# Expert transposes issued two experts ahead, a 320-column first gate product, and the order around them

## What is computed

```python
scores = jax.nn.sigmoid(tokens @ router_w)          # 64 experts, 8 chosen per token
dispatch = dispatch.at[flat_e, pos_c].add(tokens[tidx] * valid[:, None])   # 256 slots per expert
g = jnp.einsum('ech,ehi->eci', dispatch, gate_w)    # 512 -> 256
u = jnp.einsum('ech,ehi->eci', dispatch, up_w)
expert_out = jnp.einsum('eci,eih->ech', jax.nn.silu(g) * u, down_w)
contrib = gathered * (topk_w.reshape(-1) * valid)[:, None]
output = jnp.zeros((t, h), tokens.dtype).at[tidx].add(contrib)
```

## Time and profile before

| | |
|---|---|
| median of 3 runs | 1308.94 us (1308.88 to 1310.11) |
| the profiled execution, its own time | 1307.97 us |
| its span | 1306.2 us, mean granted TensorE clock 0.996 |
| busy, whole span | PE 98%, DVE 70%, ACT 50%, POOL 33% |
| chain that ended last | PE 96% |

### The profile page before, as it was taken

How to read it: one execution, slowest core, us unless ns; L and a number is a source line. 1 busy time by engine, 2 the same in 40 slices (tenths; PEclk the granted TensorE clock), 3 DMA queues, 4 the chain that set the end, 5 groups by cost and what they waited for, 6 DMA issues and landing times.

```text
span 1306.2 us, 22561 instructions
## 1 busy us (share of the span) xinstructions
PE 1280.0 (98%) x7565; PEld 1123.8 (86%) x7565; DVE 916.0 (70%) x1787; ACT 647.3 (50%) x1053; POOL 433.9 (33%) x344
## 2 busy tenths in 40 slices
PE   6999999999999999999999999999999999999995
PEld 5888888888888888888889999999999999999994
DVE  7878877777777777785656667667766766676662
ACT  4421232212322123221256777777877777777772
POOL 1000000000000000000014666777666667676653
PEclk9999999999999999999999999999999999999998
DMA  7336554664546645445447999999999999999995
GB/s 269 121 107 163 130 121 127 157 166 98 130 119 153 167 104 131 114 118 134 134 133 214 286 278 286 287 290 292 290 291 285 298 291 287 282 295 285 298 277 65
DMA packets 203800, 263.65 MB, mean 202 GB/s; under 512 B 49268, under 2 KB 138744, under 8 KB 203768
## 3 DMA queue, kind: packets, MB, share of 16 engines
q1 hardware_dynamic: 175096, 191.93, 50.9%
q0 software_dynamic: 28672, 71.32, 23.7%
HBM read 178.18 MB, written 71.39 MB: 191 GB/s over the span
## 4 chain that ended last, share of the span: by engine, by line
PE 96%; DVE 2%; DMA 1%; ACT 0%; issue 0%; POOL 0%; SPq 0%; ACTq 0%
PE pmm L1255 18%; PE pmm L1257 18%; PE pmm L1256 18%; PE pout L1255 11%; PE pout L1257 11%; PE pout L1256 11%; PE ptr L1488 4%; PE plog L1316 2%; PE plog L1325 1%; PE ptr L1267 0%; DMA out_dram<-outs,slot_cols 0%; DVE stats L829 0%; DMA xbuf<-_L_attn_proj_matrix_dram 0%; DVE xt_lo L795 0%; PE plog L1345 0%
## 5 line engine op out<-in xcount | busy, mean ns | idle before, releaser
L1614 POOL DMA_INDIRECT out_dram<-outs,slot_cols x128 | 228.7, 1787 | 165.6 <-DMA out_dram<-outs,slot_cols 136.2
L1255 PE MATMUL pmm<-xt_hi,proj_hi 128*128 128x256 f32 (+1 forms) x784 | 253.0, 323 | 2.2 <-DVE xt_lo L795 1.4
L1257 PE MATMUL pmm<-xt_hi,proj_lo 128*128 128x256 f32 (+1 forms) x784 | 249.6, 318 | 0.0
L1256 PE MATMUL pmm<-xt_lo,proj_hi 128*128 128x256 f32 (+1 forms) x784 | 249.6, 318 | 0.0
L1255 PE MATMUL pmm<-xt_hi,sgu_hi 128*128 128x256 f32 (+1 forms) x768 | 246.1, 320 | 0.2 <-issue 0.2
L1256 PE MATMUL pmm<-xt_lo,sgu_hi 128*128 128x256 f32 (+1 forms) x768 | 243.4, 317 | 0.0
L1257 PE MATMUL pmm<-xt_hi,sgu_lo 128*128 128x256 f32 (+1 forms) x768 | 243.4, 317 | 0.0
L1598 POOL TENSOR_TENSOR earlier<-earlier,chosen 128x64 bf16<-128x64 bf16 x64 | 23.9, 373 | 617.8 <-DVE chosen L916 614.0
L1604 POOL DMA_INDIRECT xbuf<-rows,slot_cols x128 | 175.3, 1369 | 80.8 <-issue 38.6
L552 ACT ACTIVATE feat<-pmm,ab 128x512 f32<-128x512 f32 x68 | 46.7, 687 | 292.4 <-PE pmm L1257 286.4
L1255 PEld LDWEIGHTS pmm<-xt_hi,proj_hi 128*128 128x128 f32 x784 | 147.3, 188 | 13.6 <-ACT feat L552 1.6
(11 more groups left out here) (185 smaller groups left out, 2543.7 us busy)
## 6 DMA issues: line engine op xcount, KB each, us to landing
raw<-in_L_ffn_gate_w_dram SPq DMA_DIRECT2D x64, 512.0 KB
raw<-in_L_ffn_up_w_dram SPq DMA_DIRECT2D x64, 512.0 KB
raw<-in_L_ffn_down_w_dram SPq DMA_DIRECT2D x64, 512.0 KB
outs<-in_L_attn_x_dram SPq DMA_DIRECT2D x32, 512.0 KB, 3.9
out_dram<-outs SPq DMA_DIRECT2D x32, 512.0 KB, 3.0
xbuf<-in_L_attn_x_dram SPq DMA_DIRECT2D x52, 256.0 KB, 7.6
raw<-xn SPq DMA_DIRECT2D x52, 256.0 KB, 6.2
rows<-raw SPq DMA_DIRECT2D x39, 256.0 KB, 4.2
```

Of the source, the lines that this page charges most:

```text
L1255: pe.matmul(psum, lh, rh, start=first and n == 0, stop=False)
L1256: pe.matmul(psum, lh, rl, start=False, stop=False)
L1257: ins = pe.matmul(psum, ll, rh, start=False, stop=final and n == len(pairs) - 1)
L1614: pool.indirect_dma_start(out=out, out_offset=bass.IndirectOffsetOnAxis(ap=slot_cols[:, at:at + 1], axis=0), in_=outs[e.b][:, c, :], in_of ...
```

## The change

On TensorE the transposes of an expert are issued two experts ahead and stand between gate-and-up products and the down products; ScalarE and VectorE handle the transposed rows at the matching place. The first gate product of every expert covers 320 columns in place of 256 (the 64 further columns are written into PSUM that the next block of products overwrites). VectorE takes `down_lo` ahead of `e_hidden` and `slot_tokens` at the front of a stage; GpSimd issues each gather one addition sooner (`add_rows(n - 5)` follows `gather(n)`).

```diff
 # ScalarE, stage
-                if next_rows:
-                    e_turned_hi(e.next())
                 if next_weights:
                     gate_up_hi(e.next())
                 e_silu(e)
                 down_hi(e)
+                if next_rows:
+                    e_turned_hi(e.next().next())
                 e_hidden_hi(e)
 # ScalarE and VectorE, start: one more e_turned_hi/lo(turn(1)) ahead of stage(turn(0))
 # VectorE, stage
-                if next_rows:
-                    e_turned_lo(e.next())
+                if tokens is not None:
+                    slot_tokens(tokens)
                 if next_weights:
                     gate_up_lo(e.next())
+                down_lo(e)
                 e_hidden(e)
-                down_lo(e)
+                if next_rows:
+                    e_turned_lo(e.next().next())
                 e_hidden_lo(e)
-                if look is not None:
-                    look[0](look[1])
+                if blocks is not None:
+                    pass_blocks(blocks)
 # TensorE, products and e_gate_up
                 for n, (lh, ll, rh, rl) in enumerate(pairs):
-                    pe.matmul(psum, lh, rh, start=first and n == 0, stop=False)
+                    if n > 0 or not lead:
+                        pe.matmul(psum, lh, rh, start=first and n == 0, stop=False)
...
+                        lead = m == 0 and i == 0
+                        if lead:
+                            pe.matmul(pmm[m][:, 0:CAP + E_LEAD], egu_hi[e.b][:, at[0]],
+                                      xt_hi[e.b][:, 0, E_COLS.start:E_COLS.stop + E_LEAD], start=True, stop=False)
 # TensorE, the loop over experts
                     e = four(2 * m + 1, k)
-                    e_turn(e.next())
                     e_gate_up(e)
                     if k == 1:
                         look_up(m + 2)
+                    e_turn(e.next().next())
                     e_down(e.prev())
 # GpSimd
-                if n >= 4:
-                    add_rows(turn(n - 4))
+                if n >= 5:
+                    add_rows(turn(n - 5))
```

More of the change, by code:

```diff
@@ L58 @@
 E_COLS = slice(48, 48 + CAP)
+E_LEAD = 64
 class Turn:
@@ L753, in _ @@
             e_turned_hi(turn(0))
+            e_turned_hi(turn(1))
             stage(turn(0), next_weights=False, out_prev=False)
@@ L761, in _ @@
             for n in range(E - 6, E - 1):
-                stage(turn(n))
+                stage(turn(n), next_rows=n < E - 2)
             stage(turn(E - 1), next_rows=False, next_weights=False)
@@ L1224, in e_hidden_lo, with stage @@
                                   ALU.subtract).then_inc(e_hid_lo_made, 1)
-            def stage(e, next_rows=True, next_weights=True, look=None):
-                if next_rows:
-                    e_turned_lo(e.next())
+            def stage(e, next_rows=True, next_weights=True, tokens=None, blocks=None):
+                if tokens is not None:
+                    slot_tokens(tokens)
                 if next_weights:
                     gate_up_lo(e.next())
+                down_lo(e)
                 e_hidden(e)
-                down_lo(e)
+                if next_rows:
+                    e_turned_lo(e.next().next())
                 e_hidden_lo(e)
-                if look is not None:
-                    look[0](look[1])
+                if blocks is not None:
+                    pass_blocks(blocks)
             e_turned_lo(turn(0))
             output(turn(GROUPS - 1), 3)
+            e_turned_lo(turn(1))
             stage(turn(0), next_weights=False)
@@ L1242, in _ @@
                 for k in range(CHUNK):
-                    stage(four(2 * m + 1, k), look=(pass_blocks, None, slot_tokens, None)[k] and (
-                        (pass_blocks, None, slot_tokens, None)[k], m + 2))
+                    stage(four(2 * m + 1, k), tokens=m + 2 if k == 2 else None, blocks=m + 2 if k == 0 else None)
             for n in range(E - 6, E - 1):
-                stage(turn(n))
+                stage(turn(n), next_rows=n < E - 2)
             stage(turn(E - 1), next_rows=False, next_weights=False)
@@ L1251, in _, with products @@
         def _(pe):
-            def products(psum, pairs, first=True, final=True):
+            def products(psum, pairs, first=True, final=True, lead=False):
                 for n, (lh, ll, rh, rl) in enumerate(pairs):
-                    pe.matmul(psum, lh, rh, start=first and n == 0, stop=False)
+                    if n > 0 or not lead:
+                        pe.matmul(psum, lh, rh, start=first and n == 0, stop=False)
                     pe.matmul(psum, lh, rl, start=False, stop=False)
@@ L1499, in e_gate_up @@
                               for h in range(HB)]
+                        lead = m == 0 and i == 0
+                        if lead:
+                            pe.matmul(pmm[m][:, 0:CAP + E_LEAD], egu_hi[e.b][:, at[0]],
+                                      xt_hi[e.b][:, 0, E_COLS.start:E_COLS.stop + E_LEAD], start=True, stop=False)
                         ins = products(pmm[m][:, i * CAP:(i + 1) * CAP], [
                             (egu_hi[e.b][:, at[h]], egu_lo[e.b][:, at[h]], xt_hi[e.b][:, h, E_COLS],
-                             xt_lo[e.b][:, h, E_COLS]) for h in range(HB)])
+                             xt_lo[e.b][:, h, E_COLS]) for h in range(HB)], lead=lead)
                     ins.then_inc((e_gate_done, e_up_done)[m], 1)
@@ L1522, in _ @@
             e_gate_up(turn(1))
+            e_turn(turn(3))
             e_down(turn(0))
@@ L1530, in _ @@
                         look_up(m + 2)
+                    e_turn(e.next().next())
                     e_down(e.prev())
             for n in range(E - 6, E - 1):
-                e_turn(turn(n + 1))
                 e_gate_up(turn(n))
+                if n < E - 2:
+                    e_turn(turn(n + 2))
                 e_down(turn(n - 1))
@@ L1627, in _ @@
                 gather(turn(n))
-                if n == 3:
+                if n == 4:
                     for b in range(2):
                         pool.wait_ge(out_stored[b], 16 * GROUPS)
-                if n >= 4:
-                    add_rows(turn(n - 4))
-            for n in range(E - 4, E):
+                if n >= 5:
+                    add_rows(turn(n - 5))
+            for n in range(E - 5, E):
                 add_rows(turn(n))
```

## The result

| | before | after |
|---|---|---|
| median of 6 runs each, same chip | 1309.53 us (1308.88 to 1310.95) | 1319.2 us (1317.24 to 1322.66) |
| ratio, 95% interval | | 1.0069 [1.0044, 1.0094] |
| profiled execution, its own time and span | 1307.97, 1306.2 us | 1319.1, 1317.4 us |

A forecast was written before the change was run, and what follows sets the result against it. TensorE was taken as the bound. Stages -12.0 us, late start +2.1, stall behind the signs +0.4 gave -9.5 from the median 1308.94: 1299.4 us, range 1297.5 to 1312.5 us.

The forecast's parts named there:

- What bounds the kernel now: Whole expert part: TensorE is the bound, 96% of the chain that ended last, busy throughout 800 to 900 us.
- The pace: Gate-and-up streams: a 320-column first product makes the other 47 take 113.4 ns each instead of 117.7; stream 5.47 us.
- the short pace: Gate-and-up products of 256 columns at 113.4 ns each; forecast for most streams, chance 0.50, total 1299.4 us.
- the long pace: Gate-and-up products of 256 columns stay at 117.7 ns each; total 1311.2 us.
- that rival: Gate-and-up streams: most stay at 117.7 ns per product, 5.67 us a stream; 1311.2 us (+0.18%), chance 0.34.
- The stage: TensorE's time per expert: ordinary 9.28 to 9.10 us, with look-up 9.81 to 9.53; 12.0 us less in all.
- The stall behind the signs: Every fourth stage, behind the sums of signs: `hid` after `sdn_lo` delays TensorE 0.03 us x 14, 0.4 us.
- The start: Expert 1's gate stream: `hid` waits behind `sdn_lo`, so TensorE starts 2.1 us later, once, never caught up.
- The additions stay each behind the landing of the one before: GpSimd's additions into the output: order and last addition stay where they were, tail unchanged, no cost.
- the transfers set the pace: Rival for all stages: transfers keep today's mean stage of 9.41 us, only the start's loss shows; 1309 to 1312 us, chance 0.08.

The follow-up runs named there:

- two chains: Odd experts' additions go into a second array, each chain waiting only for its own: changed kernel 1301.26 us (0.9914), kernel before 1305.68 us (0.9932).
- the start repaired: Changed kernel with `hid` ahead of `sdn_lo` in the first stage only: 1318.47 us (1.0075); with odd experts' additions also in a second array and chain, 1298.62 us.

## Why the prediction was wrong

**What bounds the kernel now: right, with too little said on what stood behind.** TensorE was the bound before; the run with half of the additions shows it. But 52 additions that had already waited 113.3 us were a second chain with a length of its own, close behind TensorE's, and I did not measure it as one. The trace had it: the additions of experts 10 to 55 in the kernel before start 0.5 to 3.3 us behind their rows, and a cycle has 3.92 us of issue and 5.47 of landing, 9.39 us.

**The pace: right in number, with luck, and not for the reason given.** It was called little better than even. All 48 streams whose first product took 0.147 us ran at the short pace, 47 of them in 5.49 us for 48 where 5.47 was forecast. The run without the wide product showed the long pace, 5.66 us against the 5.67 of that rival. The Trainium skill's page TensorE: Matmul & The Clock Gate, section Back-to-back issue gap, has one spacing formula, by which the wide product could win nothing; the page calls it the gap of an isolated product and says that in a stream the weight loads count too, so that the prediction held it against something that it does not describe. This case's traces have two spacings, 113.7 and 117.7 ns for 256 columns, and the wide product chose between them. The reason given, that a second product 24 ns late lets the stream set out short, did not hold: behind transposes the second product came 0.23 us after the wide one, later still, and 61 of 62 streams took the long pace.

**The stage: right in kind, a little small.** In the changed kernel with two chains the mean stage is 9.278 us against 9.399 of before with two chains: 0.121 us, times 61 is 7.4 us where 12.0 were forecast. Ordinary stages take 9.13 us (9.10 forecast) and look-up stages 9.59 (9.53): 47 x 0.03 + 14 x 0.06 = 2.3 us.

**The stall behind the signs: right in place, 0.4 forecast.** In that kernel 14 of the later streams start with a first product of 0.22 us in place of 0.15, one stage in four, and six of them then keep the long pace: 14 x 0.076 + 6 x 0.20 = 2.3 us. These 2.3 and the 2.3 above are what the 12.0 had too much. With the single chain it is much worse, and the trace shows the whole path. ScalarE, then VectorE, then TensorE, in the stage of the longest wait:

```profile
1145.30 1.27 ACT L738 ACTIVATE outs<-pout,slot_w 128x512 f32<-128x512 f32 x2 [2.58 <-DMA out_dram<-outs,slot_cols]
...
1149.18 2.23 ACT L643 ACTIVATE sgu_hi<-raw 128x1024 fp32r<-128x1024 f32 x2
1151.25 0.65 ACT L726 ACTIVATE gate_t<-pmm 128x512 f32<-128x512 f32 x1
1151.72 1.12 ACT L717 ACTIVATE sdn_hi<-raw 128x1024 fp32r<-128x1024 f32 x1
```

```profile
1152.87 1.23 DVE L1199 TENSOR_TENSOR sdn_lo<-raw,sdn_hi 128x1024 fp32r<-128x1024 f32 x1
1154.02 0.68 DVE L1220 TENSOR_TENSOR hid<-gate_t,pmm 128x512 f32<-128x512 f32 x1
```

```profile
1154.80 0.39 PE L1507 MATMUL pmm<-xt_hi,sgu_hi 128*128 128x320 f32 x1 [1.77 <-issue]
```

`outs` waits 2.58 us for a landing, the signs, the weights and the silu stand behind it, and `sdn_lo` stands ahead of `hid` as I had counted it; TensorE is idle for 1.77 us. Eleven later streams have such a gap ahead of them, 6.4 us of idle time together; counted from start to start, the down streams are 8.1 us longer in all than at their usual 2.85. All eleven resume with a first product of 0.22 us, and six of them keep the long pace, about as with two chains. This is how the chain of additions holds TensorE back: not a steady wait, but the lateness of one engine let through at its tightest stage.

**The start: an idle time of some 2.2 us forecast, 2.17 measured, and a cost that was not forecast.** The stream began 1.8 us later than before (700.06 against 698.25, 2.1 forecast), and the next one 3.6 later (710.9 against 707.3). TensorE's timeline, and then the stages view of the six microseconds that matter:

```profile
696.86 1.03 PE L1493 MATMUL ptr<-ident,xbuf 128*128 128x128 f32 x8
700.06 0.39 PE L1507 MATMUL pmm<-xt_hi,sgu_hi 128*128 128x320 f32 x1 [2.17 <-issue]
```

```profile
700.00:702.00 2.00, 1.94 (x12) 1.97 (x13) 2.00 (x4) 2.00 (x3) 1.01 (x1) 0.75 0.75 180
702.00:704.00 2.00, 2.00 (x12) 2.00 (x11) 2.00 (x2) 0.75 (x1) 1.68 (x1) 0.50 1.03 337
704.00:706.00 2.00, 2.00 (x17) 2.00 (x17) 0.07 (x1) 1.27 (x2) 0.00 (x0) 0.90 1.03 349
```

After the idle time the granted clock fell to 0.50, 1.2 GHz, and the stream took 0.22 + 6.97 us, 1.4 more than a stream that starts so and keeps the long pace (5.76). With the start repaired and two chains the granted clock is 1.00 from 698 to 706 us. With two chains the repaired start is worth 1301.26 - 1298.62 = 2.6 us; with one chain it cannot be told from nothing.

**"The additions stay each behind the landing of the one before; their last one ... is where it was, so the tail is unchanged": this is the step that failed.** Three things were wrong in it.

1. The first addition starts 6.6 us later. GpSimd's queue at the start, in the changed kernel, and ScalarE's first rows:

```profile
700.83 1.01 POOL L1615 DMA_INDIRECT xbuf<-rows,slot_cols  x1 [2.77 <-DVE slot_w L1206]
702.14 1.68 POOL L1615 DMA_INDIRECT xbuf<-rows,slot_cols  x1 [0.30 <-issue]
710.37 1.01 POOL L1615 DMA_INDIRECT xbuf<-rows,slot_cols  x1 [6.55 <-DVE slot_w L1206]
711.68 1.01 POOL L1615 DMA_INDIRECT xbuf<-rows,slot_cols  x1 [0.30 <-issue]
713.00 2.57 POOL L1625 DMA_INDIRECT out_dram<-outs,slot_cols  x1 [0.30 <-issue]
```

```profile
709.77 0.69 ACT L738 ACTIVATE outs<-pout,slot_w 128x512 f32<-128x512 f32 x1
```

The addition of expert 0 is queued behind the gather of expert 5, and that one waits 6.55 us for `slot_w`. Before, it stood ahead of that gather and went at 706.4, 0.3 us behind its first rows. The queue is only the smaller part: its rows are ready at 710.46, so it stands 2.5 us behind them, 2.3 more than before. The other 4.3 us come from the rows themselves (ready at 706.12 before): the stream of expert 1 starts 1.8 us later and takes 1.6 us longer (7.19 against 5.55), and 0.8 us of transposes now stand ahead of the down products. The runs agree: with GpSimd's old order the first addition starts at 710.0, with the start repaired at 709.1. I had counted what a gather wins by the swap, not what an addition loses, and had not carried the late start on to the additions.

2. The delay is never caught up, because a cycle of additions (9.47 us) is longer than the stage that TensorE offers (9.25). The lag is 1.2 us at the first addition and 7.0 at the fourth, and from there to the end mostly 7 to 9; the two buffers of `outs` do not let it grow further, and from then on TensorE is held to the additions' pace. The tail is 21.7 us in place of 15.3.

3. The gain of the faster stages is lost. The rival "the transfers set the pace" named this mechanism of additions behind landings, and had 0.08; what I priced was today's mean stage and the start's 2.1 us, 1309 to 1312, without the later first addition and without the stall that it feeds.

Priced by the runs: the single chain costs the changed kernel 1319.2 - 1301.3 = 17.9 us (two chips, whose kernels before had medians 0.5 us apart), of which by the traces 8.5 lie before the last product ends (1295.6 against 1287.1) and 9.3 behind it (21.7 against 12.4). It costs the kernel before 1310.07 - 1305.68 = 4.4 us, a rough figure since that kernel scattered there; the traces show 3.1 us in the tail and no change of the stage. Where the chain is out of the way, the change is worth 1301.26 - 1305.68 = -4.4 us where -9.5 was forecast, and with the start repaired -7.1 us, to be held against the forecast without the start's 2.1, -11.6. So even there the sum was some 5 us too hopeful, by the stages (4.6 us) above all.

**What stays open.** Why a first product of 320 columns picks the short pace. Why the cycle of additions is 9.47 us in the changed kernel and 9.39 before, though both wait for landings nearly every time. Why a landing takes 5.76 us beside all other transfers and 3.93 us in the tail, where no weights and no gathers are left. Neither a third of the weights less (5.58) nor half of the gathers less (5.63) brings it near. No version with the complete output was found that beats the kernel before.

## What to carry to other kernels

When the bound engine is to be made faster, write down the cycle time of every serial chain beside it (here issue plus landing, 9.47 us against a stage of 9.40), not its share of busy time and not whether the engine waits for it today: a chain within 1% of the bound took the whole gain here. When two steps of one queue swap places, price the one that moves back as carefully as the one that moves forward, at the first turn above all, since a chain without slack cannot make up for a late start. The quickest proof of a serial chain is to cut it in two with the same transfers: the bytes stay, and only the waiting goes.

## What the hardware showed that was not expected

Products of 256 columns have two paces, 113.7 and 117.7 ns, and a stream keeps the one at which it sets out; the one exception in the changed kernel's trace is the stream in which the clock fell, which came back to 2.4 GHz at the short pace. A first product of 320 columns directly behind 512-column products sets out at the short one (48 of 48); a first product of 256 there gives the long one (51 of 53), and so does the wide product behind transposes (61 of 62). Where the first product of 320 starts late and takes 0.19 to 0.22 us, either pace can follow (the long one in 8 of 14 in the changed kernel).

Additions into memory respond little when part of the load goes: with 18% less traffic (286 to 235 GB/s) their landing went from 5.76 to 5.58 us. Beside no other transfers, in the tail, it took 3.93 us. Cutting their chain in two raised the traffic to 291 GB/s.
